# Twelve blocks of the adjacency matrix transposed by DMA in two halves instead of on TensorE, their column sums added up on GpSimd

## The reference

```
h = relu(layernorm(x))
support = act_quant(relu(act_quant(h) @ weight_quant(w)))       # 4 and 3 bits
x = x + adj @ support                                            # layer 0
h = relu(layernorm(x))
A = (adj + adj.T) / 2 + I;  deg = sum(A, axis=1);  d = deg ** -0.5
x = x + (adj @ (d[:, None] * A * d[None, :])) @ h                # layer 1
```

## Time and profile before

| | |
|---|---|
| median of three runs | 529.84 us |
| the profiled execution's own time | 530.4 us |
| its span, first to last instruction | 528.6 us |
| TensorE busy | 501.2 us, 95% |
| VectorE busy | 294.6 us, 56% |
| ScalarE busy | 161.6 us, 31% |
| GpSimd busy | 1.1 us |
| DMA | 51.63 MB, mean 98 GB/s |

### The profile page before, as it was taken

How to read it: one execution, slowest core, us unless ns; L and a number is a source line. 1 busy time by engine, 2 the same in 40 slices (tenths; PEclk the granted TensorE clock), 3 DMA queues, 4 the chain that set the end, 5 groups by cost and what they waited for, 6 DMA issues and landing times.

```text
span 528.6 us, 6538 instructions
## 1 busy us (share of the span) xinstructions
PE 501.2 (95%) x2472; PEld 247.9 (47%) x2472; DVE 294.6 (56%) x417; ACT 161.6 (31%) x218; POOL 1.1 (0%) x8
## 2 busy tenths in 40 slices
PE   1577999999999999999999999999999999999997
PEld 1543565655555444444444444444444444444443
DVE  3976488899997888887789687823100100010000
ACT  1578595545463415344461212122000000000000
POOL 0000000000000000000000000000000000000000
PEclk9879999999999999999999999999999999999999
DMA  6980050353545403323232323106300010000001
GB/s 233 400 321 0 2 179 21 106 178 128 175 136 175 135 5 119 120 80 119 85 111 83 119 88 110 40 1 238 121 20 20 20 40 20 20 35 25 20 20 40
DMA packets 19250, 51.63 MB, mean 98 GB/s; under 512 B 2336, under 2 KB 2336, under 8 KB 19232
## 3 DMA queue, kind: packets, MB, share of 16 engines
q1 hardware_dynamic: 18656, 51.39, 28.4%
q10 hardware_dynamic: 576, 0.00, 0.1%
HBM read 42.99 MB, written 8.39 MB: 97 GB/s over the span
## 4 chain that ended last, share of the span: by engine, by line
PE 88%; DVE 7%; DMA 2%; ACT 2%; issue 1%; SPq 0%; ACTq 0%
PE ps_a L911 31%; PE ps_p L812 18%; PE ps_p L874 7%; PE ps_a L874 7%; PE ps_b L874 7%; PE ps_h L874 3%; PE ps_m L874 3%; PE ps_a L799 2%; PE ps_b L799 2%; DMA feat<-in_x 2%; PE ps_h L812 1%; PE ps_m L812 1%; DVE st L478 1%; DVE small L685 1%; ACT at L342 1%
## 5 line engine op out<-in xcount | busy, mean ns | idle before, releaser
L812 PE MATMUL ps_p<-small,at 128*128 128x512 f16 x448 | 102.4, 379 | 0.0
L753 DVE SCALAR_TENSOR_TENSOR feat<-ps_a,feat 128x512 f32<-128x512 f32 x16 | 11.1, 692 | 153.8 <-PE ps_a L911 153.8
L911 PE MATMUL ps_a<-small,at 128*128 128x512 f16 x384 | 85.5, 379 | 0.0
L911 PE MATMUL ps_a<-a_in,at 128*128 128x512 f16 x384 | 85.5, 379 | 0.0
L812 PEld LDWEIGHTS ps_p<-small,at 128*128 128x128 f16 x448 | 43.7, 98 | 45.4
L385 ACT ACTIVATE split<-a_in 128x1024 f16<-128x1024 f32 x30 | 31.7, 1056 | 101.9 <-PE ps_p L874 90.0
L911 PEld LDWEIGHTS ps_a<-small,at 128*128 (+1 forms) x384 | 37.6, 98 | 45.3
L911 PEld LDWEIGHTS ps_a<-a_in,at 128*128 (+1 forms) x384 | 37.6, 98 | 45.3
L681 DVE TENSOR_TENSOR split<-a_in,split 128x1024 f16<-128x1024 f32 x30 | 36.7, 1224 | 34.0 <-ACT split L385 34.0
L874 PE MATMUL ps_p<-feat,split 128*128 (+1 forms) x180 | 43.9, 379 | 0.5 <-DVE small L685 0.5
L874 PE MATMUL ps_a<-feat,split 128*128 (+1 forms) x180 | 43.7, 379 | 0.0
(11 more groups left out here) (147 smaller groups left out, 444.0 us busy)
## 6 DMA issues: line engine op xcount, KB each, us to landing
a_in<-in_adj SPq DMA_DIRECT2D x54, 512.0 KB, 3.7
out<-feat SPq DMA_DIRECT2D x32, 256.0 KB, 2.0
feat<-in_x SPq DMA_DIRECT2D x8, 512.0 KB, 11.3
at<-in_adj SPq DMA_DIRECT2D x8, 512.0 KB, 14.6
feat<-out SPq DMA_DIRECT2D x4, 1024.0 KB, 9.4
at<-in_L_gnn_weight SPq DMA_DIRECT2D x2, 512.0 KB, 5.5
split<-in_adj SPq DMA_DIRECT2D x1, 512.0 KB, 16.3
tmp<-in_adj SPq DMA_DIRECT2D x1, 512.0 KB, 17.0
```

The lines of the kernel that those rows point to most:

```text
L753: nc.vector.scalar_tensor_tensor(xr, BANK[t % 2], 1.0 / (SA * SZ), xr, ALU.mult, ALU.add)\
L812: last = nc.tensor.matmul(l0_bank(r), at_block(r, lo, j), small[:, j * D:(j + 1) * D], start=(j == 0 and lo == 0), stop=(j == T - 1 and lo ...
L911: last = nc.tensor.matmul(BANK[n], at_block(t, lo, j), z_part(j, z_lo), start=(j == 0 and lo + z_lo == 0), stop=(j == T - 1 and lo == 1))
```

## The change

Twelve odd units, 5, 7, ..., 27 (`MOVED`), are no longer turned by TensorE. ScalarE makes their high half from the unit as it lies in SBUF and gets the row sum in the same instruction (`hi_rows`). VectorE makes the low half from SBUF (`lo_rows`). Both go to a staging area of two buffers per half in `at` tile 14. SyncE's queue then issues one transposing DMA for each half, from the staging area to `at_half` (`move`). GpSimd adds the twelve units, untransposed, into one accumulator `acc` (at tile 15); TensorE turns this one sum in step 12 (`turn("acc")`), and VectorE reduces it into the column sums. `colp` is set to zero first. Row sums of moved units come out scaled by SA and are rescaled once at the end.

The PSUM turns are numbered anew (`turn_no`), since only `TURNED` units use them. Steps 1 to 11 turn one unit fewer (step 1: units 4 and 6; moved 5 and 7; from step 2 on: turned 2r+4, moved 2r+5). The row sums of the first units are spread differently (`ROW_SUMS`). The queue's order of loads, stores and transposes is written out anew. The product of step r waits for both transposes of unit 2r+1 where that is moved. ScalarE's high half of unit 28 waits for the last two moved units, whose staging area it overwrites, and `hi_rows` of a unit waits for the transposes of the moved unit two before it. The load buffers of units 10 and 11 change from tile 15 to tile 6 of `at`.

```diff
--- before.py
+++ after.py
@@ -23,6 +23,8 @@
 LATE_SUMS = (0, 1, 2, 3)
+MOVED = tuple(range(5, 28, 2))
+TURNED = tuple(u for u in range(UNITS) if u not in MOVED)
 MAGIC = 1.5 * 2.0 ** 23
@@ -87,6 +89,11 @@
         hq = [late(13, 2048 + 1024 * k, 2 * D, f16) for k in range(2)]
+        acc = late(15, 0, W, f32)
+        def stage(u, lo):
+            return late(14, 2048 * (MOVED.index(u) % 2) + lo * W, W, f16)
         xq = [late(12, 2048 * k, 2 * D, f32) for k in range(2)]
@@ -101,13 +108,21 @@
+        def turn_no(u):
+            if u == "acc":
+                return turn_no(29) + 1
+            return TURNED.index(u) + (u > 29)
         def turn_bank(u):
-            return ps_p if u < 2 else ps_b if u % 2 == 0 else ps_a
+            k = turn_no(u)
+            return ps_p if k < 2 else ps_b if k % 2 == 0 else ps_a
...
-            return 0 if u in (0, 2) else u - 1 if u > 3 else 1 if u == 1 else 0
+            k = turn_no(u)
+            return k - 1 if k > 3 else 1 if k == 1 else 0
@@ -149,6 +164,11 @@
         athi = sem("athi")
+        zeroed = sem("zeroed")
+        acc_done = sem("acc_done")
+        hi_ready = sem("hi_ready")
+        lo_ready = sem("lo_ready")
+        at_moved = [[sem(f"at_moved{k}{lo}") for lo in range(2)] for k in range(2)]
         atlo = sem("atlo")
@@ -175,7 +195,7 @@
             if RING <= u < AHEAD:
-                return late((9, 8, 7, 15)[(u - RING) // 2], u % 2 * 2 * W, W, f32)
+                return late((9, 8, 7, 6)[(u - RING) // 2], u % 2 * 2 * W, W, f32)
             return a_in[:, (u % RING) * W:(u % RING + 1) * W]
@@ -227,8 +247,19 @@
-        TURNS = {r: [2 * r + 4, 2 * r + 5] for r in range(4, T - 2)}
-        TURNS.update({1: [4, 5, 6], 2: [7, 8], 3: [9, 10, 11]})
+        TURNS = {r: [2 * r + 4] for r in range(2, 12)}
+        TURNS.update({1: [4, 6], 12: [28, 29, "acc"], 13: [30, 31]})
+        ROW_SUMS = {4: [0, 1], 6: [2, 3], 8: [4, 6], 10: [8, 10], "acc": []}
+        MOVES = {r: [2 * r + 5] if r > 1 else [5, 7] for r in range(1, 12)}
+        def wait_moved(engine, u):
+            k = MOVED.index(u)
+            for lo in range(2):
+                engine.wait_ge(at_moved[k % 2][lo], 16 * (k // 2 + 1))
@@ -244,9 +275,25 @@
             def rows_again(u):
-                sp.wait_ge(turned, before(u) + 1)
-                sp.wait_ge(rs_done, before(u) + 1)
+                free_slot(before(u))
                 rows(u)
+            def free_slot(u):
+                if u in MOVED:
+                    sp.wait_ge(lo_ready, MOVED.index(u) + 1)
+                    sp.wait_ge(acc_done, MOVED.index(u) + 1)
+                else:
+                    sp.wait_ge(turned, turn_no(u) + 1)
+                    sp.wait_ge(rs_done, TURNED.index(u) + 1)
+            def move(u):
+                for lo, ready in ((0, hi_ready), (1, lo_ready)):
+                    sp.wait_ge(ready, MOVED.index(u) + 1)
+                    if u == 13:
+                        free_slot(10 + lo)
+                    sp.dma_start_transpose(at_half(u // 2, lo, u % 2).rearrange("p (b i) -> p b i", i=P), stage(u, lo))\
+                      .then_inc(at_moved[MOVED.index(u) % 2][lo], 16)
@@ -269,14 +316,18 @@
             sums(1)
-            for u in range(AHEAD, UNITS):
+            for u in range(AHEAD, AHEAD + 4):
                 rows_again(u)
-                if u % 2 and u >= 13:
-                    store_x1((u - 13) // 2)
-            store_x1(10)
+            for r in range(1, 12):
+                if r >= 4:
+                    rows_again(2 * r + 8)
+                store_x1(r - 1)
+                for u in MOVES[r]:
+                    move(u)
+                if r >= 4:
+                    rows_again(2 * r + 9)
             for v in range(2, 6):
-                sp.wait_ge(turned, UNITS - 6 + v + 1)
-                sp.wait_ge(rs_done, UNITS - 6 + v + 1)
+                free_slot(UNITS - 6 + v)
                 sums(v)
@@ -307,6 +358,16 @@
+            nc.gpsimd.memset(colp[:, :], 0.0).then_inc(zeroed, 1)
+            for k, u in enumerate(MOVED):
+                pool.wait_ge(arr_sem(u), arrivals(u))
+                if k == 0:
+                    pool.wait_ge(lo_ready, 1)
+                    nc.gpsimd.tensor_scalar(acc, unit_in(u), 0.0, 1.0, ALU.add, ALU.mult).then_inc(acc_done, 1)
+                else:
+                    pool.wait_ge(acc_done, k)
+                    nc.gpsimd.tensor_tensor(acc, acc, unit_in(u), ALU.add).then_inc(acc_done, 1)
         @block.scalar
@@ -324,11 +385,23 @@
                 act.wait_ge(arr_sem(u), arrivals(u))
-                act.wait_ge(turned, u + 1)
+                act.wait_ge(turned, turn_no(u) + 1)
                 nc.scalar.activation(unit_in(u), unit_in(u), ACT.Copy, accum_out=rowsum[:, u:u + 1]).then_inc(rs_done, 1)
+            def hi_rows(u):
+                k = MOVED.index(u)
+                act.wait_ge(arr_sem(u), arrivals(u))
+                if k < 2:
+                    act.wait_ge(w_ready, 2)
+                else:
+                    wait_moved(act, MOVED[k - 2])
+                nc.scalar.activation(stage(u, 0), unit_in(u), ACT.Copy, scale=SA, accum_out=rowsum[:, u:u + 1])\
+                  .then_inc(hi_ready, 1)
             def hi_turned(u):
-                act.wait_ge(turned, u + 1)
+                act.wait_ge(turned, turn_no(u) + 1)
+                if u == 12:
+                    act.wait_ge(rs_done, TURNED.index(10) + 1)
                 nc.scalar.activation(at_half(u // 2, 0, u % 2), turn_bank(u)[:, :], ACT.Copy, scale=SA)\
@@ -416,16 +489,20 @@
             hi_turned(3)
-            for u in range(4, UNITS):
-                hi_turned(u)
-                if u < 8:
-                    row_sum(2 * u - 8)
-                    row_sum(2 * u - 7)
-                else:
-                    row_sum(u)
-                if u == 22:
+            for r in range(1, 14):
+                for u in TURNS[r]:
+                    if u == 28:
+                        wait_moved(act, MOVED[-2])
+                        wait_moved(act, MOVED[-1])
+                    if u != "acc":
+                        hi_turned(u)
+                    for w in ROW_SUMS.get(u, [u]):
+                        row_sum(w)
+                for u in MOVES.get(r, []):
+                    hi_rows(u)
+                if r == 9:
                     sum_hi(0)
-                if u == 26:
+                if r == 11:
                     sum_hi(1)
@@ -527,7 +604,7 @@
-                dve.wait_ge(athi, u + 1)
+                dve.wait_ge(athi, TURNED.index(u) + 1)
                 nc.vector.tensor_reduce(colp[:, u * B:(u + 1) * B],
@@ -537,7 +614,10 @@
             def lo_turned(u):
-                dve.wait_ge(athi, u + 1)
+                dve.wait_ge(athi, TURNED.index(u) + 1)
+                if u == 12:
+                    dve.wait_ge(acc_done, MOVED.index(11) + 1)
+                    dve.wait_ge(lo_ready, MOVED.index(11) + 1)
                 nc.vector.scalar_tensor_tensor(at_half(u // 2, 1, u % 2), turn_bank(u)[:, :], SA,
@@ -636,8 +716,21 @@
             def turned_out(u):
-                column_sum(u)
-                lo_turned(u)
+                if u == "acc":
+                    dve.wait_ge(turned, turn_no(u) + 1)
+                    nc.vector.tensor_reduce(colp[:, MOVED[0] * B:(MOVED[0] + 1) * B],
+                                            turn_bank(u)[:, :].rearrange("p (b i) -> p b i", i=P), AXIS.X, ALU.add)\
+                      .then_inc(atlo, 1)
+                else:
+                    column_sum(u)
+                    lo_turned(u)
+            def lo_rows(u):
+                dve.wait_ge(hi_ready, MOVED.index(u) + 1)
+                nc.vector.scalar_tensor_tensor(stage(u, 1), unit_in(u), SA, stage(u, 0), ALU.mult, ALU.subtract)\
+                  .then_inc(lo_ready, 1)
+            dve.wait_ge(zeroed, 1)
@@ -691,6 +784,8 @@
                     turned_out(u)
+                for u in MOVES.get(r, []):
+                    lo_rows(u)
                 if r - 4 in LATE_SUMS:
@@ -707,7 +802,10 @@
             rs3 = rowsum[:, :].rearrange("p (t two) -> p t two", two=2)
-            dve.wait_ge(rs_done, UNITS)
+            dve.wait_ge(rs_done, len(TURNED))
+            dve.wait_ge(hi_ready, len(MOVED))
+            moved_sums = rs3[:, MOVED[0] // 2:MOVED[-1] // 2 + 1, 1]
+            link(nc.vector.tensor_scalar(moved_sums, moved_sums, 1.0 / SA, None, ALU.mult))
             link(nc.vector.tensor_tensor(nt2[:, 0:T], rs3[:, :, 0], rs3[:, :, 1], ALU.add))
@@ -790,13 +888,17 @@
-                pe.wait_ge(arr_sem(u), arrivals(u))
+                if u == "acc":
+                    pe.wait_ge(acc_done, len(MOVED))
+                else:
+                    pe.wait_ge(arr_sem(u), arrivals(u))
                 if turn_before(u):
...
                     pe.wait_ge(sup_out, T // 2 - 3 + u)
+                source = acc if u == "acc" else unit_in(u)
                 for k in range(B):
```

(13 more changed lines are left out.)

## The result

The change makes the kernel slower: 534.67 us (median of 4 runs, 533.52 to 536.83) against 529.73 (4 runs of the kernel before), ratio 1.0101, 95% interval 1.0066 to 1.0137. The forecast was 529.7 us, no change, in a range of 523 to 562.

A forecast was written before the change was run, and what follows sets the result against it. TensorE was taken to bound the kernel, VectorE second. Turns -9.5, start stall +6.2, clock +2.4, collisions and tail +0.8 gave -0.1 us: 529.7 us, no change, range 523 to 562.

The forecast's parts named there:

- What goes: TensorE loses twelve turns and gains one: 9.5 us less; second to eleventh steps shrink from 8.65 to 7.78 us.
- The first moved unit is not hidden: Second step's products wait for unit 5, wanted at 74.33, landing at 80.5 us behind queued loads: 6.2 us stall.
- c: Transfer time of one transposing DMA of 256 KB: taken as 1.2 us, bounds 0.77 and 8.2.
- The clock: TensorE's clock falls to half behind the idle stretch at the second step's products: 2.4 us lost.
- The tail: Units 28 and 29 wait behind unit 27's transpose, but still make the turns of the sum and unit 30.
- So it fits by 0.3 us: Unit 29's low half is done at 9.2 us; the turn of unit 30 needs it at 9.5.
- collisions and the tail together: Cost of GpSimd colliding with VectorE plus the pipeline's end: 0.8 us, bounds 0 and 10.
- The prediction's own sign of being wrong: No idle stretch at 74 us, or any other TensorE idle stretch exceeding 2 us.
- The chances: Probabilities for the whole change: faster 0.30, same 0.14, slower 0.56.
- Rival 1, slow transposes: From c about 2.0 or 3.3 us every step stretches, TensorE waiting at its head: 571 to 665 us; chance 0.30.
- Rival 3, GpSimd against VectorE: Additions and low halves block each other, TensorE waits for the layer tile: about 10 us, 539 us; chance 0.13.
- the forecast's own case: No change, 529.7 us, own range 527 to 532.5; chance 0.42, split 0.15 faster, 0.14 same, 0.13 slower.
- the estimate of 10.5 us: Transfer time of one transposing DMA if its eight 128x128 blocks take 1309 ns each in a row.

The follow-up runs named there:

- the fifth experiment: Changed kernel with SyncE issuing the transposes of units 5 and 7 before the loads of units 12 to 15: 532.15 us, ratio 1.0048.
- the mended kernel: Changed kernel with unit 5 on TensorE, unit 28's waits moved and staging buffers exchanged: 524.83 us against 529.19, ratio 0.9915.

## Why the prediction was wrong, point by point

- *What goes:* right. Steps of 7.78 us, eleven turns of 0.87.
- *The first moved unit is not hidden:* right in mechanism; that the size fits is partly luck. Gap forecast 6.2, measured 5.9 us; products wanted at 74.33, at 73.94 here. The transpose is dearer than taken (c = 1.4 to 1.66, not 1.2): with c = 1.66 the forecast's own sum would have been 76.9 + 3.3 + 1.2 = 81.4, a gap of 7.1 us, so its other terms were too large. That loads ahead of it make about 2.6 us of the gap, the fifth experiment showed.
- *The clock:* right. 2.4 us taken, 9.22 - 7.07 = 2.15 measured, and gone with a busy TensorE.
- *The tail:* this step failed. "So it fits by 0.3 us" and "I take 0.8 us for collisions and the tail together"; measured 3.5 us idle and 1.7 of half clock. Two of its inputs were wrong. The low half of unit 27 was put at 7.3 us of its step, a step without lateness, though the text itself had shown VectorE even or full (7.38 and 7.8 of 7.78 us) in steps 4 to 11 and had named the collisions: it came at 9.4. And the landing was put at c + 1.2 = 2.4 us behind it: the least in the trace is 3.0, the median 3.6, here 4.5, because the queue was taken as free at that point and the issue as short (0.33 us for a load; 1.23 at least for a transpose, 2.5 here). The engines' share was 0.90 between 96.67 and 166 us, where 6.2 of 7.78 us were forecast. The slack of 0.3 us stood in the way of none of this, and the wait that turns lateness into idleness, ScalarE's in front of unit 28 with unit 29 and the sum behind it, was seen and priced at next to nothing. The prediction's own sign of being wrong, another idle stretch of TensorE over 2 us, stands exactly there. In its terms: -9.5 + 5.9 + 2.2 + 5.2 - 0.5 = +3.3 us, where it had -9.5 + 6.2 + 2.4 + 0.8 = -0.1.
- *The chances:* 0.56 were given to slower, but most of them to rivals 1 and 3, which did not come about; the forecast's own case had 0.13 for slower.
- *Rival 1, slow transposes:* its condition, c = 2.0 where the transfers decide, was missed by 0.3 us with c = 1.66; no step was stretched.
- *Rival 3, GpSimd against VectorE:* its mechanism is there and not its place. The low halves grew to 2.56 us (one of the first four to 3.39) and the sum's low half to 3.38 us, but TensorE never waited for the layer tile in the changed kernel; the lateness reached it through the tail, and in the mended kernel through the layer tile (1.0 us).
- The trace agrees with the rule of "SBUF — State Buffer" of the Trainium skill, Who interferes with whom: beside an addition these operations take up to 3.39 us, and with the additions gone they are 1.19 to 1.23 us. The Trainium skill's "Advanced Engine Details and Errata", X-Bar Transpose (TRN2), by which transposes are as fast as plain transfers, is not borne out (1.66 against 0.55 us for the same bytes). Nor is the estimate of 10.5 us from the 1309 ns of the Trainium skill's "VectorE: DVE Perf Modes", The three transpose paths: a transpose lands 3.0 us after its issue at best.

Left open: why unit 5 landed no earlier with plain copies (gap 5.9 us with both), though fewer packets were under way; why its landing came 2.7 us later in the run with a busy TensorE; and how much of the tail the order of SyncE's queue makes.

## What to carry to other kernels

When work moves from the bounding engine to a longer path, the middle of the pipeline hides it and the two ends do not: price the first unit that is wanted before the new path can deliver, and the last one, whose buffer or wait something else shares, with the lateness and the queue that the middle has by then. Put a wait in front of the one write that needs it and not ahead of an engine's whole queue. Let a helper engine start when the engine that it holds up is on work that it does not lengthen: here VectorE's late sums and its operations out of PSUM.

## What the runs showed of the hardware

- A transposing DMA of 128x1024 float16 from SBUF to SBUF is 1056 packets, takes 1.66 us of the 16 engines in the changed kernel (1.4 where only transposes were under way) and at least 1.23 us of SyncE to issue, and lands 3.0 us after its issue at best, 3.6 in the median and 6.3 at worst (9.6 in the run with the transposes before the loads). A plain copy of the same bytes: 144 packets, 0.55 us, 0.46 us to issue, 2.2, 2.6 and 6.6 us.
- GpSimd adds two 128x1024 float32 operands in 2.34 us alone, and in up to 3.4 beside a VectorE operation that reads two operands from SBUF, which itself goes from 1.2 to up to 3.4 us.
- The length of an idle stretch of TensorE did not settle by itself whether the clock fell. Idle 4.13, 3.48, 3.31 and 2.70 us (the kernel with unit 5 on TensorE, the changed one, the one with the transposes before the loads, the one without additions) was followed by a clock of about 0.50. Idle 2.89, 2.85 and 2.56 us at the tail (transposes before the loads, plain copies, busy TensorE) was followed by 12 products in 2.75 us, full clock. Where it fell at the tail, it cost 1.7 us, and 3.0 in the kernel with unit 5 on TensorE (products 4.88 instead of 2.75, turn 1.94 instead of 1.06); at the start it cost 1.7 to 2.3 us.
